# Twelve of attention group 0's maximum pieces moved into the last four projection steps of a transformer block

## The reference

```python
x = x + attn(layernorm(x)); x = x + ffn(layernorm(x))
# attn: qkv = clip(h @ Wqkv.T, -8, 8); q, k = layer_norm(q, w, b), layer_norm(k, w, b) over all 512
scores = q @ k.T / 4 + slope[head] * (key - query); scores = where(key <= query, scores, -1e30)
out = softmax(scores) @ v; return out @ Wout.T      # 32 heads of 16, S = 1024
# ffn: W_q = sum(alphas * bases, axis=0); return x @ W_q.T
```

## Time and profile before

| | |
|---|---|
| median of 3 runs | 710.57 us (710.38 to 712.33) |
| the profiled execution's own time | 710.61 us |
| its span, first to last instruction | 708.9 us |
| PE busy | 674.5 us (95%) |
| DVE busy | 575.5 us (81%) |
| ACT busy | 410.3 us (58%) |
| POOL busy | 313.2 us (44%) |
| mean granted TensorE clock | 0.966 |

### The profile page before, as it was taken

One profiled execution on the slowest core, in us unless ns is written; L12 is line 12 of the kernel. 1 busy time (PEld: TensorE's weight loads), 2 busy tenths in 40 slices (PEclk: granted clock), 3 DMA queues, 4 the chain that ended last, 5 costly groups with the idle time before them and its releaser, 6 DMA issues.

```text
span 708.9 us, 16007 instructions
## 1 busy us (share of the span) xinstructions
PE 674.5 (95%) x6096; PEld 413.3 (58%) x6096; DVE 575.5 (81%) x990; ACT 410.3 (58%) x855; POOL 313.2 (44%) x403
## 2 busy tenths in 40 slices
PE   3999999997999999999999999999999995799998
PEld 2888888884344554555455445545544431588886
DVE  6899999997999999999999999999999700367664
ACT  5132332333069887788788778878878894222221
POOL 1367766777132634626427422322232234544440
PEclk9999999997579999999999999999999999799999
DMA  8225666767945443333334334433433211544541
GB/s 303 76 61 175 179 179 187 201 192 224 289 113 134 123 128 101 115 115 106 118 108 120 108 112 123 105 108 109 130 107 105 77 26 41 154 133 131 159 146 62
DMA packets 102060, 93.64 MB, mean 132 GB/s; under 512 B 11640, under 2 KB 81912, under 8 KB 101984
## 3 DMA queue, kind: packets, MB, share of 16 engines
q1 hardware_dynamic: 97856, 86.84, 41.9%
q10 hardware_dynamic: 2016, 3.67, 1.9%
q0 software_dynamic: 2112, 2.10, 1.3%
HBM read 57.44 MB, written 33.82 MB: 129 GB/s over the span
## 4 chain that ended last, share of the span: by engine, by line
PE 73%; DVE 15%; issue 7%; POOL 2%; DMA 2%; ACT 1%; SPq 0%; DVEq 0%; POOLq 0%; ACTq 0%
PE ps L1104 23%; PE ps L1139 20%; PE ps L1084 9%; PE ps L1018 6%; PE ps L1020 5%; PE ps L1019 5%; DVE stats L957 4%; PE ps L1026 2%; DVE qk_stat L902 2%; DVE qk L898 2%; PE ps L1080 2%; DVE x_stat L868 1%; DVE xt_lo L861 1%; DVE rest L877 1%; DVE v_ext L911 1%
## 5 line engine op out<-in xcount | busy, mean ns | idle before, releaser
L957 DVE TENSOR_REDUCE stats<-ps 128x1 f32<-128x512 f32 (+3 forms) x608 | 358.3, 656 | 31.6 <-PE ps L1084 29.3
L787 ACT ACTIVATE probs<-ps 128x512 f32<-128x512 f32 (+2 forms) x640 | 309.0, 559 | 71.2 <-PE ps L1104 71.0
L1084 PE MATMUL ps<-first_k,first_q 54*128 54x128 bf16 (+3 forms) x1152 | 217.3, 282 | 5.1 <-DVE stats L957 4.5
L1104 PE MATMUL ps<-second_q,second_k 64*128 64x128 bf16 (+4 forms) x1152 | 204.6, 273 | 0.0
L1104 PE MATMUL ps<-first_q,first_k 54*128 54x512 bf16 (+3 forms) x768 | 193.8, 328 | 0.1
L679 POOL TENSOR_SCALAR_AFFINE_SELECT probs<-probs 128x256 f32<-128x256 f32 x256 | 103.0, 408 | 130.5 <-ACT probs L787 123.4
L1139 PE MATMUL ps<-probs,v_sb 128*32 128x512 f32 (+3 forms) x1536 | 157.0, 496 | 1.6 <-issue 0.8
L1104 PEld LDWEIGHTS ps<-first_q,first_k 54*128 54x128 bf16 x768 | 57.6, 94 | 110.5 <-ACT probs L787 107.6
L1084 PEld LDWEIGHTS ps<-first_k,first_q 54*128 54x128 bf16 x1152 | 92.3, 96 | 51.0 <-DVE stats L957 36.0
L1104 PEld LDWEIGHTS ps<-second_q,second_k 50*128 50x128 bf16 (+1 forms) x1152 | 91.7, 95 | 21.0 <-issue 0.6
L1018 PE MATMUL ps<-wqkv_hi,xt_hi 128*128 128x512 f32 x192 | 76.9, 401 | 0.0
(11 more groups left out here) (79 smaller groups left out, 824.4 us busy)
## 6 DMA issues: line engine op xcount, KB each, us to landing
parts_dram<-parts SPq DMA_DIRECT2D x48, 256.0 KB, 4.2
v_dram<-v_ext SPq DMA_DIRECT2D x16, 512.0 KB, 4.0
v_sb<-v_dram SPq DMA_DIRECT2D x16, 512.0 KB, 4.4
o_dram<-o_sb SPq DMA_DIRECT2D x32, 256.0 KB
first_q<-parts_dram SPq DMA_DIRECT2D x96, 64.0 KB
first_k<-parts_dram SPq DMA_DIRECT2D x96, 64.0 KB
second_q<-parts_dram SPq DMA_DIRECT2D x96, 64.0 KB
second_k<-parts_dram SPq DMA_DIRECT2D x96, 64.0 KB
```

What stands on the lines that cost most here:

```text
L787: act.activation(weights, scores, ACT.Exp, scale=SCALE).then_inc(exp_done, 1)
L957: dve.tensor_reduce(to, scores, AX.X, ALU.max).then_inc(max_taken, 1)
L1084: last = pe.matmul(ps[:, bank, r * cols:(r + 1) * cols], first_q[n % STACKS][rows, hp, i * P:(i + 1) * P], first_k[n % STACKS][rows, hp, k ...
L1104: return pe.matmul(ps[:, bank, r * cols + first:r * cols + last], stack_k[n % STACKS][rows, heads[r] // PAIR, kb * P:(kb + 1) * P], stack_ ...
```

## The change

Twelve pieces of group 0, the first twelve of `TAKES`, are scored and taken inside tile steps 12 to 15. `SOON_AT` is 12, `SOON` is 6 and `SOON_ALL` is 12.

- Pieces 0 to 5, two each in the steps 12, 13 and 14, go to the pair of QK banks of the other parity, which the previous tile's clip has freed. PE scores them between q's and k's products (`score_soon`). The next tile's QK, which writes these banks, gets a wait for their maxima.
- In step 15 pieces 6 and 7 are scored between q and k, 8 and 9 after k, 10 and 11 after v, in the ring of banks 0, 1, 2.
- DVE takes a step's two maxima just ahead of the clip L898 of that tile; in step 15 it takes 8 and 9 ahead of the clip of v, and 10 and 11 after L919.
- The waits for the cleared statistics, the masks and group 0's first stacks move with the first piece into step 12.
- `EARLY_STEPS` becomes 21, in which, without the twelve, there are 8 pieces again (12 to 19). 18 pieces are left behind the last tile step, where there were 30.

SP's, ACT's and POOL's programs stay as they are.

```diff
+SOON_AT = 12
+SOON = 2 * (TILES - 1 - SOON_AT)
+SOON_ALL = SOON + 6
+def max_bank(at):
+    if at < SOON:
+        return QK_BANK[(SOON_AT + at // 2 - 1) % 2] + at % 2
+    return MAX_BANK + at % MAX_RING
-EARLY_STEPS = 8
+EARLY_STEPS = next(v for v in range(NE) if sum(len(step) for step in PLAN[:v]) == SOON_ALL + 8)
...
 # DVE, tile_step(s)
                                       ALU.subtract, ALU.mult).then_inc(x_normed, 1)
+                if SOON_AT <= s < TILES:
+                    take_soon(2 * (s - SOON_AT))
                 t = s
                 if 0 <= t < TILES:
                     dve.wait_ge(qk_done, t + 1)
...
                     dve.bn_aggr(qk_mv[t % 2][:, 1, :], qk_stat[:, 1, :]).then_inc(qk_var, 1)
+                    if t == TILES - 1:
+                        take_soon(SOON + 2)
                     dve.wait_ge(v_done, t + 1)
...
                                       qk_rs[t % 2][:, 1:2], ALU.subtract, ALU.mult).then_inc(qk_normed, 1)
+                    if t == TILES - 1:
+                        take_soon(SOON + 4)
...
+            def take_soon(first):
+                if first == 0:
+                    dve.wait_ge(stats_cleared, 2)
+                for m, half in TAKES[first:first + 2]:
+                    take_max(0, m, half)
...
 # PE, tile_step(s)
+                    if t > SOON_AT:
+                        pe.wait_ge(max_taken, 2 * (t - SOON_AT))
                     for i in range(2):
...
+                        if i == 0 and t >= SOON_AT:
+                            score_soon(2 * (t - SOON_AT))
                     last.then_inc(qk_done, 1)
+                    if t == TILES - 1:
+                        score_soon(SOON + 2)
...
                             wqkv_hi[:, :, 2 * D:3 * D], wqkv_lo[:, :, 2 * D:3 * D]).then_inc(v_done, 1)
+                    if t == TILES - 1:
+                        score_soon(SOON + 4)
...
 # PE, score_max
-                bank = MAX_BANK + at % MAX_RING
+                bank = max_bank(at)
+                if at == 0:
+                    pe.wait_ge(masks_loaded, 16)
                 if TAKE_PLACE[m, half] == 0:
                     pe.wait_ge(first_loaded[n % STACKS], 16 * FIRST_LOADS * (n // STACKS + 1))
-                if at < MAX_RING:
+                if at < SOON:
+                    pe.wait_ge(qk_clipped, SOON_AT + at // 2)
+                elif at < SOON + MAX_RING:
                     pe.wait_ge(qk_clipped, TILES - 1)
                 else:
                     pe.wait_ge(max_taken, at - MAX_RING + 1)
```

More of the change, by code:

```diff
@@ L154 @@
 NTAKE = len(TAKES)
+XT_BANK, QK_BANK, V_BANK, QKT_BANK = 0, (1, 3), 5, 6
+EXP_BANK, PV_BANK, MAX_BANK = 3, 7, 0
+SOON_AT = 12
[5 more added lines that the diff above has]
+    return MAX_BANK + at % MAX_RING
 FIRST_STEP = -NE - EARLY
 LAST_STEP = GROUPS * NE + PV_AFTER + COPY_AFTER
-EARLY_STEPS = 8
+EARLY_STEPS = next(v for v in range(NE) if sum(len(step) for step in PLAN[:v]) == SOON_ALL + 8)
 STACKS_AT = 10
@@ L279, in build @@
         ps = ctx.enter_context(nc.psum_tensor("ps", [P, 8, BANK], F32))
-        XT_BANK, QK_BANK, V_BANK, QKT_BANK = 0, (1, 3), 5, 6
-        EXP_BANK, PV_BANK, MAX_BANK = 3, 7, 0
         O_BANK, YT_BANK, FF_BANK = (0, 1), (2, 3), (4, 5)
@@ L935, in exp_step @@
                 for m, half in PLAN[v]:
-                    dve.wait_ge(max_scored, NTAKE * n + TAKE_PLACE[m, half] + 1)
-                    take_max(n, m, half)
+                    if NTAKE * n + TAKE_PLACE[m, half] >= SOON_ALL:
+                        take_max(n, m, half)
+            def take_soon(first):
[3 more added lines that the diff above has]
+                    take_max(0, m, half)
             def take_max(n, m, half):
+                dve.wait_ge(max_scored, NTAKE * n + TAKE_PLACE[m, half] + 1)
                 segments, cols, z, diagonal = PIECES[m]
-                bank = MAX_BANK + (NTAKE * n + TAKE_PLACE[m, half]) % MAX_RING
+                bank = max_bank(NTAKE * n + TAKE_PLACE[m, half])
                 scores = ps[:, bank, 0:len(segments) * cols]
@@ L964, in _ @@
             run_tiles(dve, tile_step, -2, TILES)
-            dve.wait_ge(stats_cleared, 2)
             for s in range(FIRST_STEP, FIRST_STEP + EARLY_STEPS):
@@ L1064, in tile_step, with score_soon @@
                     turn(QKT_BANK + 1, qk[t % 2][:, 1, :], BY_HALF).then_inc(qkt_done, 1)
+            def score_soon(first):
+                for m, half in TAKES[first:first + 2]:
+                    score_max(0, m, half)
             def score_max(n, m, half):
@@ L1161, in exp_step @@
                     for m, half in PLAN[v]:
-                        score_max(n, m, half)
+                        if NTAKE * n + TAKE_PLACE[m, half] >= SOON_ALL:
+                            score_max(n, m, half)
                 if 0 <= s < GROUPS * NE:
@@ L1175, in _ @@
             run_tiles(pe, tile_step, -1, TILES - 1)
-            pe.wait_ge(masks_loaded, 16)
             for s in range(FIRST_STEP, FIRST_STEP + EARLY_STEPS):
```

## The result

The changed kernel takes 714.88 us (median of 13 executions, 712.77 to 716.55) against 711.02 us for the kernel before in the same runs: ratio 1.0052, 95% interval 1.0039 to 1.0064. It is 3.7 us slower (2.8 to 4.6). I had forecast 711.3 with a range to 713.6, so the time lies outside my range, on the side of the slower rival, near B's 713.7, yet by the mechanism of the forecast.

What follows compares the result with a forecast made beforehand. Attention was taken as PE-bound, the projections as a 9.77 us DVE loop waiting for POOL, with PE nearly full. Exp steps 0.9 us later, less 0.2 us after, gave +0.7 on 710.61: 711.3 us, range 708.0 to 713.6.

Steps and rivals of the forecast that it cites:

- B: Slower rival: steps 14 and 15 cover nothing, E moves 5.7 us, S = 202.4, +3.1 us, 713.7 us; chance 0.17.
- The two 512-wide maxima: DVE, steps 12 and 13: the maxima come wholly behind x's normalising, 1.2 us more per loop, 2.4 us in all.
- Steps 14 and 15 cover what I said: DVE idle time there absorbs part of the added maxima; idle at tile 15's clip falls from 2.69 to some 1.3 us.
- E: End of DVE's L919 of tile 15, at 166.97 us before; forecast to move 3.8 us, to 170.8.
- The join: Where DVE's maxima of group 0 end, 193.1 us before; forecast at 191.2, 1.9 us earlier.
- wout's issue: SP's load of the 1 MB wout, 186.91 us before; forecast 4.6 us later, at 191.5, landing 9.1 us afterwards.
- C: Rival: projections don't lengthen and nothing holds the shift, 6.5 us less, 704.1 us; chance 0.03.
- S: Start of the exp steps on PE, 199.3 us before; forecast 200.2, or 197.4 if nothing but the maxima decided.
- S held by wout: The forecast's mechanism: the shift waits in the DMA engines behind wout, making the exp steps 0.9 us later; chance 0.60.
- Bounds for the shift's landing: Group 0's shift DMAs: 196.1 us unhindered to 200.6 with wout's landing; 200.1 taken.
- my 0.2: Gain after the exp steps begin, with DVE's maxima ahead: 0.2 us taken, from bounds of 0 to 1.0 us.

Runs made afterwards that it cites:

- a_weights_late: Changed kernel with SP's loads of alphas and wout moved behind group 0's shift; 709.37 us, ratio 0.9977 to the kernel before.
- b_collide: Kernel before, with SP holding its loads of alphas and wout until the join of group 0's maxima, right ahead of the shift; 716.60 us, ratio 1.0092.
- a_hold: Changed kernel, with SP waiting for the shift's landing before issuing group 2's stacks; 712.73 us, ratio 1.0022 to the kernel before.
- a_ahead: Changed kernel with the maxima taken ahead of the normalising of x instead of behind it, SP's order unchanged; 711.79 us, ratio 1.0019 to the kernel before.
- a_wout_late: Changed kernel with wout alone loaded behind the shift, the alphas still ahead of it; 709.88 us, ratio 0.9977 to the kernel before.
- a_best: Changed kernel with weights behind the shift, maxima ahead of x's normalising, and maxima 8, 9 and pieces around tile 15's end retimed; 707.78 us, ratio 0.9957.
- b_weights_late: Kernel before with only SP's loads of alphas and wout moved behind group 0's shift; 711.09 us, ratio 0.9993.

## Why the prediction was wrong

**Right: everything up to the shift's issue.** The two 512-wide maxima cost each of steps 12 and 13 their 1.2 us: tile 13's clip comes at 148.5 on the old axis, 2.4 late. Steps 14 and 15 cover what I said, with 1.67 us of idle time left where I had some 1.3. E: 170.8 forecast, 170.8 measured. The join: 191.2 and 191.1. wout's issue: 191.5 and 191.7. Rivals B (E moved by 5.7 us) and C did not occur; that the time lies near B's is chance. B's own sum puts its S 0.1 us before wout's landing, where the forecast puts it 0.4 before; counted alike B would have been 0.3 us lower.

**Right: the mechanism.** "S held by wout" is what happened; a_weights_late takes the hold away and finds S where the maxima put it (197.3; 197.4 forecast), and b_collide makes it in a kernel without the change.

**Wrong: a term of the sum.** The step is "Bounds for the shift's landing: 196.1 ... to 200.6. I take 200.1". The last one landed at 204.33, 203.2 on the old axis, 3.1 us over my value and outside my bounds. wout landed at 202.0 on the old axis, not at 200.6: its 9.1 us in the kernel before became 10.3, and its issue came 0.2 us late. The shift landed 1.2 us behind it and not 0.5 ahead of it. I had even written that the last one counts, and then taken a value below wout's landing.

By the increments, 60 of 64 were in at 200.9, 0.8 us over my value; the other 2.3 us are the last four, those of the lagging engine. What I had left out is what SP issues behind the shift. Before, the stacks of group 2 (L428 then) were issued from 197.01 on, about 1 us before the shift was there; now they come, from 196.83 on, while wout and the shift are still under way in the same engines. a_hold prices that at 2.2 us of S and some 2 us of time. Without them the shift lands at 201.1, 1.0 us over my 200.1: wout lands where its 9.1 us had put it (191.8+8.7 = 200.5), the shift 0.7 us after it. Why the changed kernel's last engine lags by 2.3 us, where kernels with the same stacks behind wout show at most 0.8, stays open.

**The size of the error.** By the ratio the change costs 3.7 us, where I had 0.7; the 3.2 us by which S was too early make about the whole of this. In the profiled execution three things add up: S 3.2 us later than forecast, the start 1.1 us later, and the stretch from S to the end of the span, which is 508.6 us where it was 509.6, 1.0 us shorter and not 0.2: 711.3+3.2+1.1-0.8 = 714.8, and it took 714.9. That the last two nearly cancel is luck. The profiles of the experiments have 508.0 to 511.0 us for the stretch behind S, so my 0.2 is neither shown nor refuted.

## What to carry to other kernels

When a change pulls one transfer's producer forward and pushes another's back, look at what the transfers will stand beside, before and behind: a 4 KB DMA on the critical path took 1.8 us alone and 5 to 8 directly behind a megabyte, on either of the two queues tried, and issuing the bulk loads after it was free and turned +0.5% into -0.2%. Work added to a full loop belongs ahead of an instruction that waits for another engine, not behind it; in steps 12 and 13 it cost 1.2 us each behind it and nothing ahead of it.

## What the runs showed of the hardware

DMAs issued later can delay a small one that is still waiting behind a large one: with group 2's stacks (12 DMAs of 64 KB and 4 of 24 KB) issued behind it the shift landed 2.1 us later than with them held back (on the old axis 203.2 and 201.1), and the time was some 2 us longer. wout's own landing was 10.3 us with them and 8.7 without, but 9.0 with them in a_ahead and b_collide. A shift with nothing large ahead was not delayed by what came after it: 1.9 us for its second half in a_wout_late, with wout issued right behind.

A second queue gave the small DMA no way past: 6.2 and 6.9 us on ACT's, 6.9 and 7.2 on SP's.

A DMA is there when the slowest of its engines is: wout's last increment came 2.2 us after the 15 others in the changed kernel (203.10, 200.86), and 0.1 to 0.8 us after them in the other kernels.

The granted clock's return in the changed kernel, by windows:

```profile
208.50:209.00 0.50, 0.50 (x8) 0.29 (x5) 0.50 (x2) 0.39 (x2) 0.11 (x1) 0.50 0.00 0
209.00:209.50 0.50, 0.50 (x11) 0.32 (x7) 0.50 (x3) 0.50 (x2) 0.29 (x1) 0.99 0.00 0
```

It is back at the 2.4 GHz level 4.5 us after the first product, where PE had done nothing for 5.6 us before; in the kernel before it was between 203.0 and 203.5, some 4 us after the first product, with PE busy 5.4 of the 6 us ahead of the product. Read by quarters of a microsecond, the return comes 3.8 us (a_ahead) to 5.5 us (a_hold) after the first product where PE had waited for the shift, and 3.8 us (a_best) to 5.3 us (b_weights_late) where it had not. The hold cost little through the clock.
